# Softmax sums inverted on GpSimd ahead of their spreading, with other steps for context splits, weight stages and query parts

## What is computed

```python
xn = _layernorm(x)
q, k, v = (_split_heads(xn @ Wq.T + bq), _split_heads(ctx @ Wk.T + bk), _split_heads(ctx @ Wv.T + bv))
attn = softmax(einsum('bhqd,bhkd->bhqk', q, k) / 4, axis=-1)
x = x + einsum('bhqk,bhkd->bhqd', attn, v).transpose(0, 2, 1, 3).reshape(...) @ Wo.T + bo
# layer 1, after the scan and gelu
norm = (act - mean) / sqrt(var + 1e-5) * gamma + beta
x = x + nan_to_num(norm, nan=0.0, posinf=1e6, neginf=-1e6)
```

## Time and profile before

| | |
|---|---|
| median of 3 runs | 1099.23 us (1097.93 to 1103.1) |
| profiled execution | 1102.79 us, its span 1100.8 us |
| PE busy | 970.1 us, 88% of the span |
| DVE, ACT, POOL busy | 639.4, 554.5, 148.8 us |
| mean granted clock of TensorE | 0.953 |

### The profile page before, as it was taken

One profiled execution on the slowest core, in us unless ns is written; L12 is line 12 of the kernel. 1 busy time (PEld: TensorE's weight loads), 2 busy tenths in 40 slices (PEclk: granted clock), 3 DMA queues, 4 the chain that ended last, 5 costly groups with the idle time before them and its releaser, 6 DMA issues.

```text
span 1100.8 us, 34691 instructions
## 1 busy us (share of the span) xinstructions
PE 970.1 (88%) x15092; PEld 614.2 (56%) x15092; DVE 639.4 (58%) x1063; ACT 554.5 (50%) x1028; POOL 148.8 (14%) x182
## 2 busy tenths in 40 slices
PE   5868878988999999999997897897548999999998
PEld 2435555655665665665565565565335444445887
DVE  4745656576566656757767667665467454446342
ACT  4547566676666667456565565556247312122210
POOL 4201111121211112112121121110000000000000
PEclk9979899999999999999999999999569999999999
DMA  7585364644445442454344334322201232322210
GB/s 264 158 282 180 94 191 114 175 123 126 117 132 151 117 125 72 117 125 116 91 115 119 103 84 119 91 52 113 77 1 39 77 112 79 115 77 97 96 39 20
DMA packets 70462, 123.72 MB, mean 112 GB/s; under 512 B 34421, under 2 KB 45717, under 8 KB 67049
## 3 DMA queue, kind: packets, MB, share of 16 engines
q1 hardware_dynamic: 69480, 119.84, 37.0%
q0 software_dynamic: 544, 1.34, 0.3%
q10 hardware_dynamic: 288, 0.33, 0.1%
HBM read 64.81 MB, written 17.31 MB: 75 GB/s over the span
## 4 chain that ended last, share of the span: by engine, by line
PE 73%; DVE 13%; ACT 6%; issue 4%; DMA 2%; SPq 1%; POOL 0%; ACTq 0%; DVEq 0%
PE ps L607 71%; DVE mpart L1199 3%; ACT p L980 2%; DVE rinv L1216 2%; DVE cl L1174 2%; PE ps L858 1%; DMA stage<-in_wkv 1%; SPq L391 1%; DMA c32a<-in_ctxT 1%; ACT ch L938 1%; PE ps L742 1%; ACT kh L955 1%; ACT k L954 1%; ACT wh L991 1%; DVE oT L1219 0%
## 5 line engine op out<-in xcount | busy, mean ns | idle before, releaser
L1199 DVE TENSOR_REDUCE mpart<-ps 128x2 f32<-128x800 f32 (+1 forms) x256 | 252.7, 989 | 156.1 <-PE ps L607 155.1
L980 ACT ACTIVATE p<-ps 128x512 f32<-128x512 f32 (+1 forms) x416 | 225.5, 594 | 229.3 <-PE ps L607 228.5
L559 POOL TENSOR_TENSOR kl<-k,kh 128x400 f16<-128x400 f32 (+1 forms) x128 | 117.2, 915 | 499.0 <-ACT kh L955 499.0
L607 PE MATMUL ps<-p,v 128*17 128x64 f32 x6656 | 136.1, 226 | 6.1 <-DVE osum L1226 2.9
L1230 DVE SCALAR_TENSOR_TENSOR wl<-w,wh 128x2048 f16<-128x2048 f32 x24 | 55.0, 2292 | 125.9 <-ACT wh L991 125.9
L607 PE MATMUL ps<-kh,qbcur 64*128 64x400 f16 (+1 forms) x512 | 88.9, 345 | 41.8 <-DVE mpart L1199 38.9
L607 PEld LDWEIGHTS ps<-p,v 128*17 128x17 f32 x6656 | 101.3, 100 | 42.8 <-issue 36.6
L607 PE MATMUL ps<-wvh,ch 128*128 128x256 f16 (+1 forms) x416 | 116.2, 279 | 0.0
L607 PE MATMUL ps<-wvl,ch 128*128 128x256 f16 (+1 forms) x416 | 115.4, 277 | 0.0
L607 PE MATMUL ps<-wvh,cl 128*128 128x256 f16 (+1 forms) x416 | 115.4, 277 | 0.0
L607 PE MATMUL ps<-ch,wkh 128*128 128x400 f16 (+1 forms) x256 | 90.7, 354 | 16.0 <-DVE cl L1174 12.3
(11 more groups left out here) (206 smaller groups left out, 1390.3 us busy)
## 6 DMA issues: line engine op xcount, KB each, us to landing
ks<-kh SPq DMA_DIRECT2D x256, 100.1 KB
w<-in_wgu SPq DMA_DIRECT2D x16, 1024.0 KB, 4.8
ks<-kl SPq DMA_DIRECT2D x128, 100.1 KB
w<-in_wd SPq DMA_DIRECT2D x8, 1024.0 KB, 4.8
c32a<-in_ctxT SPq DMA_DIRECT2D x16, 400.5 KB, 4.2
cparts<-ch SPq DMA_DIRECT2D x8, 800.5 KB, 6.2
cparts<-cl SPq DMA_DIRECT2D x8, 800.5 KB, 8.1
c32a<-in_ctxT SPq DMA_DIRECT2D x12, 400.0 KB, 3.3
```

The lines of the kernel that those rows point to most:

```text
L559: nc.gpsimd.tensor_tensor(kl[:, mt, k0:k0 + w], k32[:, ku % 2, 0:w], kh[:, mt, k0:k0 + w], ALU.subtract).then_inc(sem("klo_done"), 1)
L607: return nc.tensor.matmul(o, lhsT, rhs, start=start, stop=stop, skip_group_check=shared)
L980: nc.scalar.activation(p32[0:n, step % PRING, BANK * side:BANK * side + BANK], ps[0:n, side, :], ACT.Exp, scale=DH ** -0.5).then_inc(sem(" ...
L1199: nc.vector.reduce_max(mpart[:, j0:j0 + 3:2, quarter], o.rearrange("p (b c) -> p b c", b=2)[:, :, 0:w], AX.X).then_inc(sem("max_done"), 1)
```

## The change

The softmax sums are inverted before they are spread. `take_sums` writes a second tile, `rinv`: `pvb * m + (1 - m)` with m = 1 in the rows of sums, so the other rows hold 1. POOL raises these 128x256 values to the power -1 in place (`invert_sums`, at step 2), and PE's O spreads `rinv` in place of `osum`. DVE multiplies `osum` by the spread inverses in PSUM once for all four groups, in step 4; the second half in step 5 is gone, and both reciprocals on DVE. `take_sums` moves ahead of V5, directly behind P2's maximum.

Context splits go to steps 3, 5, 7 and 9 (from 4, 6, 8, 10) with their loads one step earlier; `q_store` of the middle events goes from place 24 to 27 (from step 4 to step 7); two of the first query chains go from steps 0 and 6 of round 1 to steps 4 and 9; stages and powers go to other steps. The clean-up of the norm is written with five operations in place of seven and a memset.

```diff
--- before.py
+++ after.py
@@ -70,11 +70,11 @@
               12: ["S", "P15", "N3", "W", "T"]}
 
 WEIGH_AT = {0: (11,), 1: (12,), 3: (0, 1), **{k: (k - 2,) for k in range(4, KT)}}
-SUMS_STEP, DIVIDE_STEP = 2, 5
+SUMS_STEP = 2
 
 SECOND_BANK = ("V3", "V5", "K4", "K5", "K7", "V1", "N1", "N3")
 OWN_UNITS = ("V2", "V3", "V4", "V5", "V6")
-CTX_STEPS = {4: 0, 6: 1, 8: 2, 10: 3}
+CTX_STEPS = {3: 0, 5: 1, 7: 2, 9: 3}
 PRING = 4
 
 
@@ -83,15 +83,15 @@
 MID = {0: ["out"], 1: ["a_norm"], 2: ["a_turn"], 3: ["a_v"], 4: ["a_qk"], 5: ["a_e"], 6: ["a_p"], 7: ["a_w"],
        8: ["a_z"], 9: ["a_x"], 10: ["f_norm"], 13: ["f_turn"], 14: ["f_gate"], 15: ["f_pick"], 16: ["f_0"],
        17: ["f_1"], 18: ["f_2"], 19: ["f_3"], 20: ["f_end"], 21: ["q_norm"], 22: ["q_turn"], 23: ["q_make"],
-       24: ["q_store"]}
+       27: ["q_store"]}
 SSM = {0: ["out"], 1: ["s_norm"], 2: ["s_turn"], 3: ["s_u"], 4: ["s_0"], 5: ["s_1"], 6: ["s_2"], 7: ["s_3"],
        8: ["s_4"], 9: ["s_5"], 10: ["s_y"], 11: ["g_stats"], 12: ["g_norm"], 13: ["g_clean"], 14: ["m_stats"],
        15: ["m_norm"], 16: ["m_turn"], 17: ["r_logits"], 18: ["r_pick"]}
 QUERIES = ["q_stats", "q_norm", "q_turn", "q_make", "q_store"]
-FIRST = {(0, 0): 1, (1, 0): 2, (1, 6): 3}
+FIRST = {(0, 0): 1, (1, 4): 2, (1, 9): 3}
 STAGE_JOBS = 8
-STAGE_AT = {(0, 3): 1, (0, 5): 2, (0, 7): 3, (0, 9): 4, (0, 12): 5, (1, 7): 6, (1, 12): 7}
-POWERS_AT = {(0, 6): 0, (0, 8): 1, (0, 10): 2, (0, 11): 3, (1, 5): 4}
+STAGE_AT = {(0, 2): 1, (0, 6): 2, (0, 8): 3, (0, 10): 4, (0, 12): 5, (1, 1): 6, (1, 10): 7}
+POWERS_AT = {(0, 7): 0, (0, 9): 1, (0, 11): 2, (0, 12): 3, (1, 0): 4}
 SPLIT_AT = {(G - 1, 9): 0, (G - 1, 11): 1}
 
 
@@ -160,7 +160,7 @@
     i = int(name[1:] or 0)
     return {"K": ("khi_done", K_UNITS * r + i + 1), "N": ("khi_done", K_UNITS * r + i + 1),
             "V": ("v_done", V_UNITS * r + i + 1), "P": ("max_done", 2 * NP * r + i + 1),
-            "T": ("row_done", r + 1), "O": ("oT_done", 2 * r + 2)}[name[0]]
+            "T": ("row_done", r + 1), "O": ("oT_done", r + 1)}[name[0]]
 
 
 def event_read_by(name, layer, t):
@@ -264,6 +264,7 @@
         rows = sb(ctx, "rows", [P, 4, D])
         sel = sb(ctx, "sel", [P, P])
         half = sb(ctx, "half", [P, 1])
+        minus = sb(ctx, "minus", [P, 1])
         bT = sb(ctx, "bT", [P, KC, N])
         cT = sb(ctx, "cT", [N, D])
         rw = sb(ctx, "rw", [P, KC, 2, E])
@@ -276,7 +277,7 @@
         prt = sb(ctx, "prt", [P, 3 * TT, 2])
         cmb = sb(ctx, "cmb", [P, 3 * TT, E])
         cmb2 = sb(ctx, "cmb2", [P, 3 * TT, E])
-        SM_IOTA, SM_MIX, SM_HEAD = 2, 10, 18
+        SM_IOTA, SM_MIX, SM_HEAD, SM_SUM = 2, 10, 18, 22
 
         with ExitStack() as s:
             am = sb(s, "am", [N, 6, 2, N])
@@ -504,9 +505,9 @@
                         restack(g + 1, 1)
                         if g + 2 < G:
                             load_high_queries(g + 2)
-                    if k in (5, 7) and g + 2 < B:
+                    if k in (4, 6) and g + 2 < B:
                         load_ctx(4 * (g + 2) + k // 2)
-                    if k in (9, 11) and g + 3 < B:
+                    if k in (8, 10) and g + 3 < B:
                         load_ctx(4 * (g + 3) + k // 2 - 4)
                     if k in (4, 6) and B <= g + 2 < G:
                         load_parts(g + 2, k // 2 - 2)
@@ -567,6 +568,14 @@
                           "m_stats": "m_"}[name]
                     inverse_root(stats_index(to, 1, t))
 
+            def invert_sums(r):
+
+                pool.wait_ge(sem("o_copied"), r + 1)
+                sums = rinv[:, :, :].rearrange("p g q -> p (g q)")
+                nc.gpsimd.tensor_tensor(sums, sums, minus[:, 0:1].broadcast_to([P, GROUPS * NQ]), ALU.pow)\
+                  .then_inc(sem("inverse"), 1)
+
+            nc.gpsimd.memset(minus[:, :], -1.0)
             nc.gpsimd.memset(half[:, :], -0.5).then_inc(sem("half_ready"), 1)
             nc.gpsimd.memset(qcur[0][:, :, :], 0.0)
             nc.gpsimd.memset(qcur[1][:, :, :], 0.0).then_inc(sem("qcur_zero"), 1)
@@ -592,8 +601,11 @@
                     for name in STEP_UNITS[k]:
                         if name[0] in "KN" and has_unit(name, g):
                             klo(round_of(name, g), int(name[1]))
+                    if k == SUMS_STEP and g:
+                        invert_sums(g - 1)
                     for name, layer, t in events(g, k):
                         event(name, layer, t)
+            invert_sums(G - 1)
             for name, layer, t in LAST:
                 event(name, layer, t)
             for it in range(IT):
@@ -670,8 +682,8 @@
 
             def o_unit(r):
 
-                pe.wait_ge(sem("o_copied"), r + 1)
-                mm(mid[:, 0:GROUPS * NQ], sel[:, :], osum[:, :, :].rearrange("p g q -> p (g q)"), True,
+                pe.wait_ge(sem("inverse"), r + 1)
+                mm(mid[:, 0:GROUPS * NQ], sel[:, :], rinv[:, :, :].rearrange("p g q -> p (g q)"), True,
                    True).then_inc(sem("o_mm"), 1)
 
             def run_unit(name, r, prologue=False):
@@ -744,7 +756,7 @@
                 elif name == "out":
                     if t == 0:
                         pe.wait_ge(sem(f"wo{layer}_in"), 16)
-                    pe.wait_ge(sem("oT_done"), 2 * (B * layer + 2 * t + 2))
+                    pe.wait_ge(sem("oT_done"), B * layer + 2 * t + 2)
                     for e in range(GROUPS):
                         last = mm(mid[:, 0:D], oT[:, e, :], wo[:, e, :], e == 0, e == GROUPS - 1)
                     last.then_inc(sem("xo_mm"), 1)
@@ -1189,7 +1201,7 @@
                         rows[0:n, 3, :].rearrange("p (h d) -> p h d", h=H).unsqueeze(1)
                         .broadcast_to([n, len(kts), H, DH]), ALU.mult, ALU.add).then_inc(sem("v_done"), 1)
                 elif letter == "O":
-                    divide(r, 0)
+                    divide(r)
                 elif letter == "P":
                     j0, quarter = pairs_and_quarter(i)
                     w = QUARTERS[quarter][1]
@@ -1208,22 +1220,22 @@
                     nc.vector.tensor_scalar(m16[:, :], m32[:, :], 1 / M_SCALE, None, ALU.mult)\
                       .then_inc(sem("m_ready"), 1)
 
-            def divide(r, half):
-
-                two = slice(2 * half, 2 * half + 2)
+            def divide(r):
+
                 dve.wait_ge(sem("o_mm"), r + 1)
                 need(dve, "xo_mm", r // 2)
-                nc.vector.reciprocal(rinv[:, two, :], mid[:, 2 * NQ * half:2 * NQ * half + 2 * NQ]
-                                     .rearrange("p (g q) -> p g q", g=2)).then_inc(sem(f"o_inverse{half}"), 1)
-                dve.wait_ge(sem(f"o_inverse{half}"), r + 1)
-                nc.vector.tensor_tensor(oT[:, two, NQ * (r % 2):NQ * (r % 2) + NQ], osum[:, two, :],
-                                        rinv[:, two, :], ALU.mult).then_inc(sem("oT_done"), 1)
+                nc.vector.tensor_tensor(oT[:, :, NQ * (r % 2):NQ * (r % 2) + NQ], osum[:, :, :],
+                                        mid[:, 0:GROUPS * NQ].rearrange("p (g q) -> p g q", g=GROUPS),
+                                        ALU.mult).then_inc(sem("oT_done"), 1)
 
             def take_sums(r):
 
                 dve.wait_ge(sem("pv_mm"), KT * (r + 1))
-                need(dve, "oT_done", 2 * r)
-                nc.vector.tensor_copy(osum[:, :, :], pvb).then_inc(sem("o_copied"), 1)
+                need(dve, "oT_done", r)
+                nc.vector.tensor_copy(osum[:, :, :], pvb)
+                need(dve, "o_mm", r)
+                nc.vector.tensor_scalar(rinv[:, :, :], pvb, small[:, SM_SUM:SM_SUM + 1], small[:, SM_SUM + 1:SM_SUM + 2],
+                                        ALU.mult, ALU.add).then_inc(sem("o_copied"), 1)
 
             def split_w(w):
                 dve.wait_ge(sem("whi_done"), w + 1)
@@ -1363,16 +1375,15 @@
                     if t == 0:
                         dve.wait_ge(sem("gamma_in"), 16)
                     link(nc.vector.tensor_tensor(g_a[:, :], g_n[:, :], rows[:, 0, :], ALU.mult))
-                    link(nc.vector.memset(g_z[:, :], 0.0))
                     link(nc.vector.tensor_tensor(g_n[:, :], g_a[:, :], rows[:, 1, :], ALU.add))
                 elif name == "g_clean":
                     link(nc.vector.tensor_scalar(g_f[:, :], g_n[:, :], 0.0, 0.0, ALU.mult, ALU.is_equal))
-                    link(nc.vector.copy_predicated(g_z[:, :], g_f[:, :], g_n[:, :]))
-                    link(nc.vector.tensor_scalar(g_m[:, :], g_n[:, :], F32_MAX, CLAMP, ALU.is_gt, ALU.mult))
-                    link(nc.vector.tensor_tensor(g_z[:, :], g_z[:, :], g_m[:, :], ALU.add))
-                    link(nc.vector.tensor_scalar(g_m[:, :], g_n[:, :], -F32_MAX, -CLAMP, ALU.is_lt, ALU.mult))
-                    link(nc.vector.tensor_tensor(g_z[:, :], g_z[:, :], g_m[:, :], ALU.add))
-                    link(nc.vector.tensor_tensor(xt, xt, g_z[:, :], ALU.add))
+                    nc.vector.tensor_scalar(g_m[:, :], g_n[:, :], F32_MAX, None, ALU.is_gt)
```

(19 more changed lines are left out.)

## The result

The changed kernel took 1674.53 us (median of 4 runs, 1672.55 to 1675.93) against 1099.74 for the kernel before in the same comparison: ratio 1.522, 95% interval 1.518 to 1.526. The forecast of 1080, and its range to 1145, missed by far, and in sign. Rival B, at 0.18, is what happened. The profiled execution took 1674.55 us, its span 1672.7.

What follows compares the result with a forecast made beforehand. PE was taken to bound the kernel, so DVE savings count only where PE waits. Terms of -17.1, -2.6, -1.6, -11.4, -1.3 and +2.2 sum to -31.8 us, two thirds kept (-21), forecast 1080 us, range 1068 to 1145.

Steps and rivals of the forecast that it cites:

- Rival B: POOL's power takes over 8 us (over 30 ns a column) and PE waits: 1140 us and up; chance 0.18.
- the lower end: POOL's power on 256 columns: dear part paid once, each column priced as in a subtraction, 1.1 us.
- What covers the power: From masked copy to spreading matmul, 4.1 to 5.2 us; a power up to about 4.0 us is free.
- It costs about 15 us for each us beyond: PE's wait at the spreading matmul in 15 rounds if the power outlasts 4.2 us.
- DVE's saving: Division on DVE falls from 3.27 to 1.24 us a round, 32.5 us less busy time over 16 rounds.
- The P6 and P8 waits: PE's waits after DVE's division in steps 4 and 5: ten at P6 go, -17.1; two at P8, -2.6.
- the three terms' 21.3: PE's waits at P6 (-17.1), at P8 (-2.6) and behind the norm's clean-up (-1.6).
- Context splits, -11.4: N2's waits for the fourth context split in rounds 0 to 5 go when it moves to step 9: -11.4 us.
- Stage one step earlier, +2.2: Second layer's weight stage at step 2: its DMA landing is fixed, so PE stops earlier and loses 2.2 us.
- The tail: Last division, running alone, from 4.3 to 3.8 us; with the last clean-up, 0.8 shorter, -1.3.
- All PE gaps over 0.3 us between 47 and 765 us come to some 62 us: Main loop: the most that any rearrangement of it can give.
- I count two thirds as kept: -21: Of the summed -31.8 us, because gaps are not independent and an earlier PE meets the next late thing.

Runs made afterwards that it cites:

- the run with the product: Changed kernel with POOL's power replaced by a product of the same shape (sums not inverted, output wrong): 1061.85 us, ratio 0.9625.
- the moves: Changed kernel's moved steps and short clean-up, with the division on DVE as before: 1073.5 us, ratio 0.9738 to the kernel before.
- the new division alone: Kernel before with only the new form of the division, a product in place of POOL's power (output wrong): 1087.93 us, ratio 0.9852.
- the turning: Changed kernel without POOL's part: PE turns the sums to 128 x 8, DVE inverts and widens them, PE spreads: 1069.81 us, ratio 0.9702.
- 64 columns: Changed kernel with the power on 64 of 256 columns, other sums uninverted: 1184.37 us, ratio 1.0731 to the kernel before.

## Why the prediction was wrong

The step that failed is the price of the power: "I take the lower end, since the subtraction is the nearest row for what a wide instruction costs per column". The lower end was 1.1 us and the truth 41.14, with 0.159 us a column against 0.0021. The two bounds, 1.1 and 115 us, did hold it. The row that should have had more weight is the power on one column: 0.55 us against 0.098 for a memset. Of that excess about a third (0.159) recurs at each column and the rest is paid once, which no row told. But even a tenth of the excess at each column would have been 11.5 us, near three times what was covered. So the split of chances, 0.46 for nearly all of it being paid once, was not what the row bore out, and a range that left out case B was too narrow on that side. The other price that the prediction looked at, twice the two reciprocals or 3.8 us, was as far off: the power took over 21 times their 1.90 us.

Point by point:

- What covers the power: 4.1 to 5.2 us forecast, up to 4.0 free. In the 15 rounds of the loop it was 3.6 to 5.0. Right; and at 2.9 us PE waited in none of them.
- "It costs about 15 us for each us beyond": by this the 41.14 us would have given about 1634; it was 1674.5. The sixteenth place, behind the loop and uncovered, is missing from the formula: the waits are 592 us over the product and not 554. The clock, which the forecast set aside as not touched, is the second error, 22 us. Against both stand the gains, some 18 us larger than forecast.
- DVE's saving: 32.5 us forecast. 45.7 us of reciprocals and products gave way to 6.7 for the product and 8.6 for the masked copy, so 30.4. The masked copy was 0.54 us, not 0.41.
- The P6 and P8 waits: in the timeline of the run with the product none of them over 0.3 us is left, so -17.1 and -2.6 were right; the two waits behind the clean-up fell from 2.11 to 0.81, so 2.6 for 1.6. PE's waits for `mpart` fell by 22 us, from 38.9 to 16.8, but that this is near the three terms' 21.3 is chance: 6.5 of it is the stage's wait, which is now one for the exponentials (those rose from 10.5 to 21.5), and new waits for the maximum behind the split and the query store of step 7 came up, 7.5 us in seven rounds. The first line is the stage's wait, the second the longest of step 7:

```profile
68.15 0.61 PE L619 MATMUL ps<-qcur,ks 64*128 64x64 f16 x16 [8.53 <-ACT p L992]
...
263.47 0.34 PE L619 MATMUL ps<-kh,qbcur 64*128 64x400 f16 x2 [2.45 <-DVE mpart L1211]
```

- Context splits, -11.4: 17 us measured alone, with an interval that holds 11.4; its waits fell from 12.3 us to 1.3 there and 2.6 in the kernel with the product. In both, two short ones of the six in the loop are left, so "the wait is gone" holds for four.
- Query stores out of step 4: 8 us by putting them back, which the forecast had inside the 17.1. Of these 17.1 the moves took the larger part: 4.1 are left with them alone, 12.3 with the new division alone.
- Stage one step earlier, +2.2: too small for the times, but in the traces the wait grew from 6.45 to 8.53 us with the product, as forecast. Clean-up, -2.4: too small to be told by the times.
- The tail: 4.3 us before; 3.8 forecast with a power of 1.1. With the product's 0.61 it took 3.4. Right.
- "All PE gaps over 0.3 us between 47 and 765 us come to some 62 us", and no rearrangement could give more: they come to 72, and the second half is wrong too, as the next point shows.
- "I count two thirds as kept: -21": for the waits this was near the mark. With the power out of the way the span was 1058.5, 42.3 us under before; of that PE's idle time is 25.4 (130.7 to 105.3), four fifths of the 31.8. The next late things were met, at step 7 above all. The other 16.9 us are PE's busy time (970.1 to 953.2), which no term of the forecast had. They lie in the main loop, before and then with the product:

```profile
53.00:778.00 725.00, 645.36 (x13165) 422.97 (x13163) 457.71 (x803) 445.49 (x888) 118.68 (x140) 0.96 0.45 126
```

```profile
53.00:738.00 685.00, 629.65 (x13141) 415.84 (x13140) 423.97 (x765) 443.04 (x884) 128.21 (x154) 0.98 0.46 132
```

The work is nearly the same, at a mean granted clock of 0.98 in place of 0.96. By the clock records 47.4 us of PE's busy time in the loop stood at half clock before and 17.6 with the product; half of the difference is 14.9 us, near the 15.7 by which busy time in the loop fell. So a removed wait gave back more than its length, as an added one took more. Each of these figures is from one trace, and the mean clock moves between runs of one kernel too (0.947 to 0.960 in seven runs of the kernel before), so the size is good to some us only.

## What to carry to other kernels

A price with a range of a hundred to one and a cover of 4 us in it is not a detail of the sum: the forecast is that price, and the chances have to be spread over the range by what the nearest row of the same operation shows, not by a different operation of the same width. Before an operation with a high price per column goes to another engine, make it narrow: the same 1024 sums were 256 columns on four useful partitions, or eight on 128; and count what the turning costs the engine that does it (10.1 us of PE here). And a stall on TensorE cost its length and, behind it, 3 to 6 us at half clock, so the sum of the waits was not a bound on what taking them away gave.

## What was not expected of the hardware

- `pow` on POOL: 0.159 us a column for 1, 16, 64 and 256 columns, plus 0.39; a product of the same shape 0.612 us in all for 256 columns. With DVE's reciprocal at 0.95 us for 128 columns (7.4 ns a column), the power is some 21 times dearer per column. Its time did not vary: all 16 on 256 columns took 41.14 us within 1 ns.
- A product on POOL with a broadcast operand took 2.4 ns a column, a subtraction of two full tiles 2.3 (0.914 us for 400).
- Stalls of 6.5 us and of 37 us were followed by the same stretch at half clock, 4.6 us on average (3.1 to 6.4).
- A DVE addition of two SBUF tiles took 1.11 us beside a subtraction on POOL, 0.43 alone, and 0.42 beside the power: a busy POOL alone did not slow it.
- In the changed kernel 6 norms waited for their inverse root behind the power in POOL's queue (152 us of DVE's idle time). No cost of it is seen: PE stood still anyway, and the remainder of the span is 22.1 us, as with 64 columns (21.4), where these waits come to 30.
